# Six small operations of the gates and the layer norm, moved from DVE to POOL in the MoE parts

## The reference

```
x = x + 0.5 * ffn(layernorm(x), Wg, We, be)
x = x + attn(layernorm(x), Wq, Wk, Wv, Wo, Wf)
x = x + 0.5 * ffn(layernorm(x), Wg, We, be)

def ffn(x, Wg, We, be):            # 8 experts, the best 2 of each token
    probs = softmax(x @ Wg)
    top_vals, top_idx = top_k(probs, 2)
    gates = top_vals / sum(top_vals)
    expert_out = einsum('th,ehd->etd', x, We) + be[:, None, :]
    return sum(gates[..., None] * expert_out[top_idx, tok, :], axis=1)
```

## Time and profile before

| | us |
|---|---|
| median of 3 runs | 492.1 (491.86 to 494.57) |
| the profiled execution | 494.02, its span 492.3 |
| first MoE part, up to where attention alone runs | about 0 to 100 |
| second MoE part by itself | about 410 to 492 |

### The profile page before, as it was taken

The page is one execution under the profiler, slowest core; times in us unless marked ns, Lnnn a source line. Parts: engine busy times, 40 slices in busy tenths (PEclk is TensorE's granted clock), DMA queues, the critical chain, the costliest instruction groups (busy, mean ns, idle before and its releaser), DMA issues.

```text
span 492.3 us, 12103 instructions
## 1 busy us (share of the span) xinstructions
PE 424.1 (86%) x3488; PEld 309.6 (63%) x3488; DVE 370.6 (75%) x1316; ACT 274.4 (56%) x757; POOL 242.5 (49%) x398
## 2 busy tenths in 40 slices
PE   0688888766899999999999999999999989888884
PEld 0566666535676766766676676676667657666662
DVE  2999999975657866865775686676667637999996
ACT  3366676440255664565565456455555765766753
POOL 9775556352135434533534543553443443566554
PEclk9999999885689999999999999999999989999999
DMA  3211000023342333233233233323322000000101
GB/s 108 89 52 20 1 0 1 1 91 110 87 117 75 109 101 103 84 97 116 69 99 105 76 100 99 100 85 98 115 75 72 3 3 0 23 24 21 43 22 43
DMA packets 29402, 32.47 MB, mean 66 GB/s; under 512 B 2312, under 2 KB 26140, under 8 KB 29370
## 3 DMA queue, kind: packets, MB, share of 16 engines
q1 hardware_dynamic: 28282, 31.57, 22.1%
q10 hardware_dynamic: 1088, 0.52, 0.4%
HBM read 16.05 MB, written 15.20 MB: 63 GB/s over the span
## 4 chain that ended last, share of the span: by engine, by line
PE 42%; DVE 20%; DMA 18%; issue 10%; ACT 4%; POOL 3%; DVEq 1%; SPq 1%; ACTq 0%; POOLq 0%
DMA a_q_rows<-a_max_t 14%; PE bank L809 10%; PE bank L824 8%; DVE m_lower L278 6%; PE bank L839 6%; PE bank L812 5%; DVE m_stats L305 2%; PE bank L930 2%; PE bank L925 2%; PE bank L922 2%; DMA q_stage<-a_q_parts 2%; POOL m_pair L216 2%; DVE x_all L287 2%; PE bank L848 1%; DVE m_best_no L346 1%
## 5 line engine op out<-in xcount | busy, mean ns | idle before, releaser
L735 DVE TENSOR_REDUCE a_neg_max<-bank 128x2 f32<-128x512 f32 (+1 forms) x192 | 124.5, 686 | 77.9 <-PE bank L812 77.5
L674 ACT ACTIVATE a_weights<-bank 128x512 f32<-128x512 f32 x192 | 108.2, 591 | 60.7 <-PE bank L824 56.0
L620 POOL TENSOR_SCALAR_AFFINE_SELECT a_weights<-a_weights 128x512 f32<-128x512 f32 (+1 forms) x96 | 75.7, 789 | 127.7 <-ACT a_weights L674 127.7
L809 PE MATMUL bank<-a_k_rows,a_q_rows 104*128 104x256 f32 (+1 forms) x512 | 103.2, 327 | 5.8 <-DMA a_k_rows<-k_stage 4.9
L809 PEld LDWEIGHTS bank<-a_k_rows,a_q_rows 104*128 104x128 f32 x512 | 81.3, 203 | 25.3 <-issue 18.2
L241 ACT ACTIVATE m_scaled<-bank,m_gates 128x128 f32<-128x128 f32 x256 | 72.5, 366 | 26.8 <-PE bank L387 26.8
L824 PE MATMUL bank<-a_q_rows,a_k_rows 106*128 106x512 f32 (+1 forms) x192 | 70.7, 447 | 11.9 <-DMA a_q_rows<-a_max_t 9.8
L216 POOL TENSOR_TENSOR m_pair<-m_scaled 128x256 f32<-128x256 f32 x64 | 48.5, 758 | 62.4 <-ACT m_scaled L241 62.3
L278 DVE SCALAR_TENSOR_TENSOR m_lower<-bank,m_gates,m_lower 128x128 f32<-128x128 f32 x192 | 65.5, 341 | 1.2
L812 PE MATMUL bank<-a_mask,a_ident 128*128 128x256 bf16 (+1 forms) x192 | 64.3, 335 | 0.0
L839 PE MATMUL bank<-a_weights,a_v 128*32 128x128 f32 x1536 | 62.1, 280 | 0.0
(11 more groups left out here) (121 smaller groups left out, 785.5 us busy)
## 6 DMA issues: line engine op xcount, KB each, us to landing
a_k_rows<-k_stage SPq DMA_DIRECT2D x16, 416.0 KB
k_stage<-a_k_parts SPq DMA_DIRECT2D x48, 128.0 KB
q_stage<-a_q_parts SPq DMA_DIRECT2D x48, 128.0 KB
a_q_rows<-q_stage SPq DMA_DIRECT2D x64, 96.0 KB
x_all<-in_L_attn_x SPq DMA_DIRECT2D x8, 256.0 KB, 2.7
out_x<-x_all SPq DMA_DIRECT2D x8, 256.0 KB, 2.3
we<-in_L_ffn_We SPq DMA_DIRECT2D x1, 512.0 KB, 3.9
k_stage<-a_c_parts SPq DMA_DIRECT2D x32, 16.0 KB
```

The costliest lines, as they stand in the source:

```text
L620: nc.gpsimd.affine_select(out=diagonal, in_=diagonal, compare_op=ALU.is_ge, fill=0.0, base=0, pattern=[[0, heads.stop - heads.start], [1, P]],
L674: nc.scalar.activation(weights[n // 2 % 3][:, half:half + 4, :].rearrange("p h n -> p (h n)"), wt_bank[n % 2][:, :], ACT.Exp).then_inc(wt_ ...
L735: nc.vector.tensor_reduce(neg_max[:, t, first:first + heads], score_bank[p % 2][:, :].rearrange("p (h n) -> p h n", h=heads), AX.X, ALU.ma ...
L809: nc.tensor.matmul(bank[:, n * keys:(n + 1) * keys], q_rows[b][0:KR, h, t * P:(t + 1) * P], k_rows[b][0:KR, h % NU, 0:keys], start=n == 0, ...
```

## The change

POOL takes over in q = 0 the eps addition (var_eps) and the negated mean (neg_mean), behind add_upper and ahead of rstd, and in q = 3 the product of hot and g12, the gate sum, the high part (now as an addition of zero) and the low part, behind add_upper of tile 3. Each of the moved operations waits on a semaphore for the one before it. DVE keeps the rest of the chain, and CH goes from 8 to 5. In front of the next one-hot pattern DVE waits for gates_done, so that it doesn't overwrite hot. Nothing else moves.

```diff
--- before.py
+++ after.py
@@ -194,7 +194,9 @@
     y_ready, high_used = sem("y_ready"), sem("high_used")
     low_chain, pair_done, upper_done, upper_used = sem("low_chain"), sem("pair_done"), sem("upper_done"), sem("upper_used")
     stored, waited = sem("stored"), sem("waited")
-    CH = 8
+    neg_done, hot_done, pool_waited = sem("neg_done"), sem("hot_done"), sem("pool_waited")
+    gates_done, gates_hi_done = sem("gates_done"), sem("gates_hi_done")
+    CH = 5
 
     def load_group(sp, g):
 
@@ -222,14 +224,31 @@
 
         def part(i, s, q):
             N, B, b, n = s + 2 < G, 0 <= s, s % 2, i + 3
+            A, a, m = -1 <= s and s + 1 < G, (s + 1) % 2, i + 2
+            flat = gates[:, a].rearrange("p q e -> p (q e)")
             if B:
                 add_upper(i, q)
             if q == 0 and N:
+                wait_apart(pool, mom_done, n, pool_waited)
+                nc.gpsimd.tensor_scalar(var_eps[:, b], moments[:, b, :, 1], EPS, None, ALU.add).then_inc(eps_done, 1)
+                nc.gpsimd.tensor_scalar(neg_mean[:, b], moments[:, b, :, 0], -1.0, None, ALU.mult).then_inc(neg_done, 1)
                 pool.wait_ge(eps_done, n)
                 nc.gpsimd.tensor_tensor(rstd[:, b], var_eps[:, b], c["minus_half"][:, 0:Q],
                                         ALU.pow).then_inc(rstd_done, 1)
+                pool.wait_ge(neg_done, n)
                 pool.wait_ge(rstd_done, n)
                 nc.gpsimd.tensor_tensor(shift[:, b], neg_mean[:, b], rstd[:, b], ALU.mult).then_inc(shift_done, 1)
+            if q == 3 and A:
+                pool.wait_ge(chain, (m - 1) * CH + 5)
+                nc.gpsimd.tensor_tensor(hot[:, :, :, :], hot[:, :, :, :],
+                                        g12[:, :, :].unsqueeze(3).broadcast_to([P, 2, Q, E]), ALU.mult).then_inc(hot_done, 1)
+                pool.wait_ge(hot_done, m)
+                nc.gpsimd.tensor_tensor(gates[:, a], hot[:, 0], hot[:, 1], ALU.add).then_inc(gates_done, 1)
+                wait_apart(pool, gates_done, m, pool_waited)
+                nc.gpsimd.tensor_scalar(gates3[:, 0:3:2], flat.unsqueeze(1).broadcast_to([P, 2, Q * E]), 0.0, None,
+                                        ALU.add).then_inc(gates_hi_done, 1)
+                pool.wait_ge(gates_hi_done, m)
+                nc.gpsimd.tensor_tensor(gates3[:, 1], flat, gates3[:, 0].bitcast(FP32), ALU.subtract).then_inc(gates_ready, 1)
         return part
 
     def scalar(act):
@@ -293,9 +312,6 @@
         def part(i, s, q):
             N, A, B = s + 2 < G, -1 <= s and s + 1 < G, 0 <= s
             a, b, m, n = (s + 1) % 2, s % 2, i + 3, i + 2
-            flat = gates[:, a].rearrange("p q e -> p (q e)")
-
-
             if q == 0 and N:
                 if x_dram is not None:
                     dve.wait_ge(x_in, m * 16)
@@ -317,10 +333,6 @@
                 if q == 0:
                     dve.wait_ge(bias_added, i + 1)
                 expert(i, s, q, 0)
-            if q == 0 and N:
-                dve.wait_ge(mom_done, m)
-                nc.vector.tensor_scalar(neg_mean[:, b], moments[:, b, :, 0], -1.0, None, ALU.mult)
-                nc.vector.tensor_scalar(var_eps[:, b], moments[:, b, :, 1], EPS, None, ALU.add).then_inc(eps_done, 1)
             if q == 1 and A:
                 wait_apart(dve, logits_ready, n, waited)
                 for k in range(Q):
@@ -329,14 +341,12 @@
             if q == 2 and A:
 
                 dve.wait_ge(no_ready, n)
+                at_least(dve, gates_done, n - 1)
                 nc.vector.tensor_tensor(hot[:, :, :, :], every, best_no[:, :, 0:2].rearrange("p q r -> p r q").unsqueeze(3)
                                         .broadcast_to([P, 2, Q, E]), ALU.is_equal)
 
                 dve.wait_ge(egap_ready, n)
                 nc.vector.tensor_scalar(denom[:, :], egap[:, :], 2.0, 2.0, ALU.mult, ALU.add).then_inc(chain, 1)
-            if q == 3 and A:
-                after_link(n, 6)
-                nc.vector.tensor_tensor(gates[:, a], hot[:, 0], hot[:, 1], ALU.add).then_inc(chain, 1)
             if B:
                 expert(i, s, q, 1)
             if q == 1 and A:
@@ -348,14 +358,8 @@
             if q == 2 and A:
                 after_link(n, 3)
                 nc.vector.reciprocal(g12[:, 0], denom[:, :]).then_inc(chain, 1)
-            if q == 3 and A:
-                after_link(n, 7)
-                nc.vector.tensor_copy(gates3[:, 0:3:2], flat.unsqueeze(1).broadcast_to([P, 2, Q * E])).then_inc(chain, 1)
             if B:
                 expert(i, s, q, 2)
-            if q == 3 and A:
-                after_link(n, 8)
-                nc.vector.tensor_tensor(gates3[:, 1], flat, gates3[:, 0].bitcast(FP32), ALU.subtract).then_inc(gates_ready, 1)
             if q == 3 and N:
                 dve.wait_ge(hi_ready, m)
                 nc.vector.tensor_tensor(xt_lo[:, b], xt_bank[:, :], xt_hi[:, b].bitcast(FP32), ALU.subtract).then_inc(lo_ready, 1)
@@ -366,10 +370,6 @@
                 nc.vector.tensor_tensor(g12[:, 1], egap[:, :], g12[:, 0], ALU.mult).then_inc(chain, 1)
             if B:
                 expert(i, s, q, 3)
-            if q == 2 and A:
-                after_link(n, 5)
-                nc.vector.tensor_tensor(hot[:, :, :, :], hot[:, :, :, :],
-                                        g12[:, :, :].unsqueeze(3).broadcast_to([P, 2, Q, E]), ALU.mult).then_inc(chain, 1)
             if q == 3 and s == G - 1:
                 finish(G * Q - 1, 1)
         return part
```

## The result

The changed kernel takes 557.7 us (median of four runs, 554.9 to 558.5) beside 492.4 for the kernel before on the same chip: 1.130 times the time, 95% interval 1.125 to 1.134. The profiled execution took 558.5 with a span of 556.8, the kernel before 494.0 with 492.3. The forecast was 545, with a range of 526 to 557. The result lies at the upper edge of that range: 557.7 as measured, or 556.0 if the ratio is taken of the 492.1 from which the forecast starts.

What follows compares the result with a forecast made beforehand. DVE was busiest (9.86 of 10 us), but a loop through four engines, with the gates last at PE, was taken to decide. 492.1 + 41 (queue, seventh handovers, start) + 12 (clock) = 545 us, range 526 to 557.

Steps and rivals of the forecast that it cites:

- The signs: Groups of 13 to 15 us, PE's gate turn waiting over 3 us for POOL, DVE share about 0.65, clock under 1.00.
- The queue, 41 us: Gates behind POOL's tile 3 sums lengthen each handover by 2.98 us; with start and seventh handovers 41 us, clock unchanged.
- A turn of 13.09: One loop through four engines, from bias matmul to bias matmul: 13.09 us after the change, against 10.11 before.
- The pause of PE: PE has nothing to do from the end of the next group's tile 0 to the gates: 3.8 us a group.
- The seventh handovers: Last passage between groups in each MoE part: 2.2 us more in the second part, 0.3 (0 to 2.9) in the first.
- the start: POOL waits for the first group's gates before filling the third attention buffer, delaying its first pair sum: 3.0 us (1 to 4).
- The clock, 12 us: PE runs at half clock behind its pause in each group: +1.0 us a group (0 to +1.9), 12 us in all.
- (a): Rival: PE's clock stays full despite the pauses, 533 us (527 to 543); chance 0.30.
- (b): Rival: the gates are not last at PE, so DVE's 0.95 us a group count, 13 us less: 479; chance 0.05.
- (c): Rival: POOL's folded patterns cost 1 us each, 4.4 for the four gate operations, 34 us more: 579; chance 0.04.
- (d): Rival: POOL and DVE hold each other up; no cost on the loop, or 549 if 0.3 us a group; no chance given.
- Eps and negated mean: Behind add_upper on POOL they make rstd some 0.2 us later, hidden behind maxima and gap; without that cover 2.4 us.

Runs made afterwards that it cites:

- the kernel with the filled pause: The changed kernel with ten extra 128x512 matmuls on PE ahead of its wait for the gates, in most groups: 534.5 us, 1.086.

## Why the prediction was right, and where its size was off

**What bounds it.** Right: the gates were last at PE, and the new place behind add_upper put them 3 us later. Moving the block by one call took 53 of 65 us away, which shows that the place and not the amount of work is the cause. The signs came too: PE's turn waited 3.2 us for POOL, DVE's bias add 3.0 us, DVE's busy share in the middle of both parts was 0.63 (0.65 forecast), and the clock there was 0.76 to 0.78. Only the group, 15.15 us in the mean, lay just above the 13 to 15.

**The queue, 41 us.** Right, term by term. A turn of 13.09 was forecast with the clock full, and 12.96 measured in the kernel with the filled pause (13.13 with the first one). Its steady turns have 3.27 to 3.32 to the maxima (3.33) and 5.93 to 6.20 on to ACT's end (5.92). The whole was 42.8 us (534.5 less 491.7) against 41. The four gate operations took 1.49 (forecast 1.60), inside their bounds. The pause of PE was forecast with 3.8 us and is 2.4 to 3.2.

**The seventh handovers and the start.** In the kernel with the fillings the second part's seventh costs 11.79 - 9.50 = 2.3 (forecast 2.2). The first part's costs 0.9 there (0.3), with its own pause not filled. POOL's first pair sum came at 27.77 (27.4), the fill at 19.43 (19.0).

**The clock, 12 us.** This is the term that was mis-sized: 22.5 us by the medians (65.3 less 42.8), 2.02 a handover and not 1.0, just above the upper end of 1.9 that I had given. I had reckoned that a part of the low stretch would fall into the pause and that PE would be slow for the turn and part of tile 1. That was the step that failed. Every turn but the first of each part has all six matmuls of tile 1 at 0.63 us, which is +1.41 up to the maxima, and about every other one has the logits and tile 2 slow as well, +2.54 (5.87 against 3.33). In addition 0.4 to 0.5 us is lost between the maxima and ACT's end (6.29, and 6.40 in the next turn, against 5.92). The clock's 10.5 us beyond the 12, with 1.8 of the queue, are the distance from 545 to the result.

**Rivals.** (a) 533 with the clock full is what the filled kernel gave, 534.5; in the changed kernel the clock did fall. (b) had a second fault besides its condition: it priced the six operations at 0.95 us a group. With the work gone entirely a group gains 0.35, and the kernel 0.7%. The distances between DVE's steps were read rightly, but what is late next was not asked for: PE's fourth tile and POOL's holds. So 479 is out of reach for this move as long as the rest of the order stays as it is. (c) is refuted, the folded pattern took 0.30. (d) In the changed kernel it costs nothing on the loop, as said; in the kernels without the long wait it matters: with eps and the negated mean on POOL it goes with the difference between 1.009 and 1.000.

**Eps and negated mean.** That the later rstd is hidden was right, but the forecast saw only rstd's readers. Alone the move costs 1.009. In the profiled execution the span is 3.8 longer: 0.6 at the start, 2.1 in the twelve groups, about 1 less in the first part's seventh and 2.1 more by the start of the second part; the last two lie beside attention, and what made them stays open.

The attention between the two parts took nearly the same time in both kernels: the last bias add of the first part comes 30.9 us later than before, and the first of the second part 30.2.

## What to carry to other kernels

Before work goes to an engine with room, write down what stands ahead of it in that engine's queue and when that is released: the same six operations cost 65 us with four of them behind one wait and 13 with these ahead of it, and none of the three places tried made the kernel faster. Then leave the work out altogether, once, to see what the move could bring at best; here it was 0.7%. And where a loop through several engines gets a long pause on PE, count at least the whole dense piece behind the pause that stands on the loop at the slow clock; here it was tile 1 in nearly every turn, and the logits and tile 2 as well in about every other.

## What the runs showed of the hardware that was not expected

**DVE and POOL keep each other out, and who starts first wins.** A finish of DVE (two inputs in SBUF) takes 0.27 us when it starts 0.01 ahead of POOL's pair sum and 0.77 when it starts 0.10 behind it; the sum then takes 0.86 or 0.72. So 0.1 us of phase is worth 0.5 us on DVE, and 0.24 us less work can cost time. The fourteen traces agree on this pair of operations, and the border is sharp. All 116 finishes that begin 0.03 to 0.55 us behind a pair sum end 0.13 to 0.17 us behind it. All 142 that begin between 0.02 behind it and 0.20 ahead of it take 0.27 to 0.29 us, and the sum takes up to 0.89. The Trainium skill (GPSIMD Engine Reference, section 8) says that POOL shares its SBUF interfaces with DVE and contends with DVE's two-port modes and with two SBUF inputs. The trace agrees for the two-input finish; it shows besides that DVE's operation then ends just behind POOL's. One-input operations are held too, and whether they run in a two-port mode no trace shows: the copy above (0.55), and, at the start of the kernel before, DVE's denominator:

```profile
16.71 3.61 DVE L336 TENSOR_SCALAR m_denom<-m_egap 128x4 f32<-128x4 f32 x1
```

It works on 4 elements and ends at 20.32, with POOL's fill, 16.79 + 3.51. Here DVE's row begins 0.08 ahead of POOL's and DVE is held all the same, so for this pair of operations the recorded starts do not tell who wins; what does was not tried.

**One input on POOL was not cheaper.** On POOL, by form (count, busy us, mean ns, idle before):

```profile
L248 POOL TENSOR_SCALAR m_gates<-m_gates 128x64 fp32r<-128x64 f32 x16 | 6.2, 385 | 3.1 <-POOL m_gates L246 3.1
L243 POOL TENSOR_TENSOR m_hot<-m_hot,m_g 128x64 f32<-128x64 f32 x16 | 4.7, 295 | 0.1
```

The high part has one tensor input and takes 385 ns, the product of two inputs of the same size 295. The prediction had weighed the Trainium skill's statement that one-input work is roughly at line rate (GPSIMD Engine Reference, section 4.1), by which it would have been the cheaper; this case's rows speak against it at this size, though the high part also converts its output and reads a folded pattern. Without either, at 128x4, the one-input operations took 225 and 227 ns (L233, L234) and the two-input shift 200 (L240).

**The clock's low stretch has two lengths in turn.** In the changed kernel pauses of PE of 2.6, 3.2 and 2.5 us ended with the gates' turns at 52.99, 67.67 and 83.64. Around them the granted clock was 0.50, that is 1.2 GHz, from about 53.6 to 57.0, from 67.3 to 77.4 and from 84.3 to 87.7 us:

```profile
56.00:57.00 1.00, 1.00 (x5) 0.76 (x3) 0.96 (x4) 0.00 (x0) 0.84 (x4) 0.51 0.00 0
57.00:58.00 1.00, 1.00 (x12) 1.00 (x10) 0.51 (x2) 0.86 (x4) 0.85 (x2) 1.00 0.00 0
...
76.00:77.00 1.00, 1.00 (x4) 0.76 (x3) 0.35 (x2) 0.95 (x4) 0.00 (x0) 0.50 0.00 0
```

What makes a stretch short or long was not tried. In the kernel with the gates ahead of tile 3's sums PE still pauses 1.0 to 1.1 us for them in the steady groups, and the clock there is 1.00. Near its start, though, the clock fell to 0.50 at 35 us, behind pauses of 1.09, 1.18 and 0.44 us that stand close together. Pauses of little over 1 us were thus followed by either level.
